# A decoder layer with attention, feature mixing and 64 experts on one core: queries copied by transfers, projection work dealt anew, and rest blocks of 64 rows with both parts in one product

## The reference: what is computed

```
x: (4, 1024, 1024) float32, ctx: (4, 1024, 512)
x = x + attention(layernorm(x))      # 16 heads of 64, causal, rotary positions
x = x + mixing(layernorm(x), ctx)    # softmax(q k^T) of ctx, applied to x (one per sequence)
x = x + experts(layernorm(x))        # 64 experts, top 8, inner width 384
# experts:
top_val, top_idx = top_k(softmax(x @ gate.T), 8)
# the lower four choices of a token may be rerouted to a similar expert that some token has among its first four
rerouted = mapping[top_idx];  rerouted[:, :4] = top_idx[:, :4]
# rows are grouped by expert, with group_sizes counted from the data
gate, up = split(ragged_dot(xs, gate_up_proj));  y = ragged_dot(silu(gate) * up, down_proj)
out[tok] += y * w
```

## Time and profile before

| what | time |
|---|---|
| median of the runs | 7708.29 us |
| the profiled execution | 7711.42 us |
| its span (first to last instruction) | 7709.8 us |
| its mean granted TensorE clock | 0.969 |

### The profile page before, as it was taken

One profiled execution on the slowest core, in us unless ns is written; L12 is line 12 of the kernel. 1 busy time (PEld: TensorE's weight loads), 2 busy tenths in 40 slices (PEclk: granted clock), 3 DMA queues, 4 the chain that ended last, 5 costly groups with the idle time before them and its releaser, 6 DMA issues.

```text
span 7709.8 us, 118231 instructions
## 1 busy us (share of the span) xinstructions
PE 7148.1 (93%) x37743; PEld 5881.9 (76%) x37744; DVE 3972.6 (52%) x7056; ACT 3523.7 (46%) x6510; POOL 1815.6 (24%) x1602
## 2 busy tenths in 40 slices
PE   7998888898996899995799999999999999999999
PEld 5776776776775778784688888888888888888887
DVE  5666667666665443445444444444444444444444
ACT  4666676666665222120244444444444444444443
POOL 1122113113110000000233333333333333333333
PEclk9999999999998999996899999999999999999999
DMA  2111111112111222221465555556556565556555
GB/s 66 45 55 51 44 55 51 44 45 60 45 46 58 79 69 85 76 67 36 123 176 170 161 161 161 161 161 165 161 155 165 161 181 160 159 163 162 162 161 150
DMA packets 303596, 858.60 MB, mean 111 GB/s; under 512 B 42080, under 2 KB 83552, under 8 KB 303328
## 3 DMA queue, kind: packets, MB, share of 16 engines
q0 software_dynamic: 98928, 365.58, 20.3%
q1 hardware_dynamic: 204400, 489.67, 19.5%
HBM read 614.84 MB, written 206.70 MB: 107 GB/s over the span
## 4 chain that ended last, share of the span: by engine, by line
PE 52%; DVE 0%; POOL 0%; issue 0%; DMA 0%; ACT 0%; DVEq 0%; POOLq 0%
PE ps_gu L1932 10%; PE ps_gu L1934 10%; PE ps_gu L1933 10%; PE ps_y L1932 5%; PE ps_y L1934 5%; PE ps_y L1933 5%; PE ps_xe L1952 3%; PE ps_xe L1961 1%; PE ps_l L1941 1%; PE ps_h L2044 0%; DVE logits L2206 0%; DMA x_rows<-rows,gather_s 0%; DVE xs_lo L2252 0%; DVE at_hi L2199 0%; POOL x_rows L1869 0%
## 5 line engine op out<-in xcount | busy, mean ns | idle before, releaser
L1932 PE MATMUL ps_gu<-xs_hi,gu_hi 128*128 128x512 f32 x3072 | 1213.5, 395 | 7.3 <-DVE gu_lo L2291 7.3
L1934 PE MATMUL ps_gu<-xs_hi,gu_lo 128*128 128x512 f32 x3072 | 1207.0, 393 | 0.0
L1933 PE MATMUL ps_gu<-xs_lo,gu_hi 128*128 128x512 f32 x3072 | 1204.4, 392 | 0.0
L1911 POOL TENSOR_TENSOR dn_lo<-raw_w,dn_hi 128x512 fp32r<-128x512 f32 x384 | 485.0, 1298 | 947.0 <-ACT dn_hi L2114 947.0
L1932 PEld LDWEIGHTS ps_gu<-xs_hi,gu_hi 128*128 128x128 f32 x3072 | 577.8, 188 | 130.4 <-DVE gu_lo L2291 7.7
L461 PE MATMUL ps_qkv<-xt_hi,w_hi 128*128 128x512 f32 x1512 | 639.8, 423 | 37.7 <-ACT proj L614 30.0
L1933 PEld LDWEIGHTS ps_gu<-xs_lo,gu_hi 128*128 128x128 f32 x3072 | 578.1, 188 | 124.8
L1934 PEld LDWEIGHTS ps_gu<-xs_hi,gu_lo 128*128 128x128 f32 x3072 | 577.6, 188 | 125.3
L1932 PE MATMUL ps_y<-dn_hi,hs_hi 128*128 128x512 f32 x1536 | 628.6, 409 | 0.0
L893 DVE TENSOR_TENSOR pt_lo<-ps_t,pt_hi 128x512 fp32r<-128x512 f32 (+3 forms) x768 | 426.6, 555 | 391.9 <-ACT pt_hi L713 376.9
L644 ACT ACTIVATE probs<-ps_s,neg_max 128x128 f32<-128x128 f32 (+7 forms) x512 | 379.5, 741 | 506.6 <-DVE neg_max L824 505.7
(11 more groups left out here) (326 smaller groups left out, 15577.1 us busy)
## 6 DMA issues: line engine op xcount, KB each, us to landing
raw_w<-w_gu SPq DMA_DIRECT2D x384, 512.0 KB, 4.2
raw_w<-w_down SPq DMA_DIRECT2D x192, 512.0 KB, 6.3
w_raw<-wqkv SPq DMA_DIRECT2D x192, 256.0 KB, 2.7
turned<-proj SPq DMA_DIRECT2D x512, 64.0 KB, 2.0
out<-residual SPq DMA_DIRECT2D x36, 512.0 KB, 2.6
attn_out<-out_t POOLq DMA_DIRECT2D x128, 128.0 KB, 2.3
residual<-x SPq DMA_DIRECT2D x32, 512.0 KB, 5.3
stage<-attn_out SPq DMA_DIRECT2D x32, 512.0 KB, 5.8
```

Of the source, the lines that this page charges most:

```text
L1911: pool.tensor_tensor(dn_lo[:, f, a], raw_w[:, f, a], raw(dn_hi[:, f, a]), ALU.subtract).then_inc(dn_lo_ok, 1)
L1932: pe.matmul(out, a_hi, w_hi, start=first, stop=False)
L1933: pe.matmul(out, a_hi, w_lo, start=False, stop=False)
L1934: return pe.matmul(out, a_lo, w_hi, start=False, stop=last)
```

## The change

**Attention.**

- `twin_queries` moves from VectorE to the SP queue: two transfers from `q_hi` to `q_hi` for each half of the queries, ordered at the step in which ScalarE rounds them. `split_queries` waits for both.
- A table `SHARE` says how many of the 144 projection matmuls stand in each of the 24 steps, in place of six in each. A chain can end at other steps (`ended`), and the emptying of the bank and the rotation's transfers follow it.
- The fourth query block of each unit (`ON_DVE = (3,)`) is multiplied with its reciprocal by VectorE, directly after the reciprocal, and no more by ScalarE. TensorE waits on two semaphores for a unit.
- The other tables are changed. SP's and GpSimd's lists are made from the tables step by step.

**Experts.**

- Rest blocks have 64 rows (`T = P // 2`). Their number is counted anew: the part of ceil(count / 64) above 8. The held operand has the high parts of the 64 rows in its first 64 columns and the low parts in the other 64 (`xt`, `ht`), so a product is two matmuls: with the high and with the low weights. The result has two halves of 64 partitions, and they are added: for gate and up ScalarE copies the lower half out (`lower_rows`) and VectorE adds (`add_rows`). To the second layer's output both halves are added in `out`: by `send_last` for the first 64 partitions and `send_second` for the others, which waits until the first has landed.
- The table has each rest block's row numbers twice (`finish_list`); `scatter_n`, `scatter_l` and `scatter_m` hold them for the sends (`place_last`).
- In a rest block the second layer's first part stands before the third transpose, and ScalarE's and VectorE's third h behind the next tail's rows.
- ScalarE splits the first two chunks of the next expert's weights before it reads the counts (`first_weights`).

```diff
@@ self_attention
-    PER = NS // NC
+    TERMS = 3 * HB
...
-    SCALED_AT = {False: (5, 9, 15, 18), True: (5, 9, 17, 21)}
-    ADDED_AT = {False: (6, 10, 16, 19), True: (6, 10, 18, 21)}
-    HI_AT = {False: (6, 10, 16, 20), True: (6, 10, 18, 21)}
-    LO_AT = {False: (7, 11, 17, 21), True: (7, 11, 19, 22)}
-    TWIN_AT = {False: {15: 1, 22: 3}, True: {15: 1, 22: 3}}
-    V0_AT = {False: 21, True: 15}
-    V1_AT = 3
-    W_AT = {4: (1, 4), 5: (1, 5), 18: (2, 0), 19: (2, 1), 22: (2, 2), 23: (2, 3)}
+    SHARE = {False: [6, 6, 6, 6, 5, 3, 9, 7, 6, 6, 6, 6, 11, 13, 2, 6, 5, 2, 5, 4, 7, 6, 6, 5], True: [8, 8, 8, 6, 6, 6, 6, 6, 6, 6, 6, 8, 7, 9, 6, 6, 6, 6, 4, 4, 4, 4, 4, 4]}
+    SCALED_AT = {False: (4, 8, 13, 17), True: (5, 10, 14, 20)}
+    ADDED_AT = {False: (5, 10, 14, 19), True: (6, 11, 17, 20)}
+    HI_AT = {False: (6, 10, 17, 19), True: (7, 11, 20, 21)}
+    LO_AT = {False: (7, 11, 18, 20), True: (8, 12, 21, 21)}
+    V0_AT = {False: 23, True: 15}
+    V1_AT = 1
+    W_AT = {2: (1, 4), 6: (1, 5), 15: (2, 0), 18: (2, 1), 22: (2, 2), 23: (2, 3)}
     XN = GQ
-    X_AT = {6: ((13, 14), (16, 17), (18, 19), (20, 22)), 7: ((2, 3), (4, 5), (6, 7), (8, 9))}
+    ON_DVE = (3, )
+    X_AT = {6: ((12, 13), (16, 17), (18, 19), (20, 23)), 7: ((0, 3), (4, 5), (6, 7), (8, 9))}
...
+            def twin_queries(j, p, n):
+                half = chains_of(p)[turns_of(p)[n]][1]
+                a = slice(half * HALF, half * HALF + HALF)
+                sp.wait_ge(qk_hi_ok, START + j * 4 + n + 1)
+                sp.dma_start(raw(q_hi[HD:P, 0, a]), raw(q_hi[0:HD, 0, a])).then_inc(twin_ok, 16)
+                sp.dma_start(raw(q_hi[0:HD, 1, a]), raw(q_hi[HD:P, 1, a])).then_inc(twin_ok, 16)
...
+                if i in ON_DVE:
+                    dve.wait_ge(inv_ok, START + j * NQ + n + 1)
+                    stand_alone(dve, passed)
+                    dve.tensor_scalar(probs[g][:, i, 0:keys], probs[g][:, i, 0:keys], inv_sum[:, n:n + 1], 1.0,
+                                      ALU.mult, ALU.mult).then_inc(norm_late, 1)
@@ experts
+            def send_second(n):
+                pool.wait_ge(yl_sent, LOADED + n * 32 + 16)
+                stand_alone(pool, passed)
+                pool.indirect_dma_start(out, bass.IndirectOffsetOnAxis(ap=scatter_m[:, 0:1], axis=0), y_last[T:P, :], None,
+                                        compute_op=ALU.add).then_inc(yl_sent, 16)
...
+            def packed_product(out, a, w_hi, w_lo, first, last):
+                both = a.rearrange("p a t -> p (a t)")
+                pe.matmul(out, both, w_hi, start=first, stop=False)
+                return pe.matmul(out, both, w_lo, start=False, stop=last)
...
+            def place_last(n):
+                dve.wait_ge(yl_sent, LOADED + n * 32)
+                dve.wait_ge(wl_ok, START + n + 1)
+                stand_alone(dve, passed)
+                dve.tensor_copy(scatter_m[:, :], scatter_n[T:P, :])
+                dve.tensor_copy(scatter_l[:, :], scatter_n[:, :]).then_inc(sl_ok, 1)
...
             def tail_block(e, t):
+                def add_rows(f):
+                    dve.wait_ge(tlow_ok, START + t * FB + f + 1)
+                    dve.tensor_tensor(gu_sum[:, f % 2, :], ps_gu[0:T, f % 2, 0:W], gu_low[:, f % 2, :], ALU.add).then_inc(tsum_ok, 1)
...
                 gather_tail_index(e + 1 + t, (e + 1) * SUP + t + 1)
+                place_last(e + 1 + t)
+                add_rows(0)
                 multiply(0)
+                add_rows(1)
                 multiply(1)
                 rest_of_h(0)
+                add_rows(2)
                 multiply(2)
                 rest_of_h(1)
-                rest_of_h(2)
...
                 keep_tail_weights(e + 1 + t, e)
                 rest_of_tail(e + 1 + t)
-                dve.wait_ge(yl_sent, LOADED + (e + t + 2) * 16)
-                stand_alone(dve, passed)
-                dve.tensor_copy(scatter_l[:, :], table[:, bass.ds((e + 1) * SUP + t + 1, 1)]).then_inc(sl_ok, 1)
+                rest_of_h(2)
```

More of the change, by code:

```diff
@@ L156, in at_border, with share, ended @@
         return p % NP >= NP - 2
+    def share(p, s):
+        before = sum(SHARE[at_border(p)][:s])
+        return [(n // TERMS, n % TERMS) for n in range(before, before + SHARE[at_border(p)][s])]
+    def ended(p, s):
+        return [c for c, n in share(p, s) if n == TERMS - 1]
     def chains_in(p):
@@ L353, in attention @@
-                if exists(j + 2):
-                    load_w(j + 2, p + 2, 4)
-                    load_w(j + 2, p + 2, 5)
-            for_pairs(sp, lambda: None, attention, lambda: None)
+                for s in range(NS):
+                    if not last:
+                        for n in range(4):
+                            if s == HI_AT[border][n] and chains_in(p)[turns_in(p)[n]][0] == Q:
+                                twin_queries(j + 1, p + 1, n)
+                    if more and p == NP - 2:
+                        for t in range(GQ):
+                            if s == X_AT[p][t][1]:
+                                load_next(b, t + XN)
+                    if s in W_AT:
+                        ahead, i = W_AT[s]
+                        ahead, i = (ahead, i + RAWS) if i + RAWS < NC else (ahead + 1, i + RAWS - NC)
+                        if exists(j + ahead):
+                            load_w(j + ahead, p + ahead, i)
+                    if not last:
+                        for c in ended(p, s):
+                            if c in turns_in(p):
+                                turn_halves(j + 1, c, turns_in(p).index(c))
@@ L358, in _, with prologue @@
+            def prologue():
+                turn_halves(0, 0, 0)
+                turn_halves(0, 1, 1)
+                twin_queries(0, 0, 1)
+                turn_halves(0, 3, 2)
+                load_w(1, 1, 0)
+                load_w(1, 1, 1)
+                turn_halves(0, 4, 3)
+                twin_queries(0, 0, 3)
+                for i in range(RAWS, NC):
+                    load_w(1, 1, i)
+            for_pairs(sp, prologue, attention, lambda: None)
             for k in range(RAWS):
@@ L551, in attention @@
                         scores(j + ahead, (slot + ahead) % 2, unit, i)
-                    if 0 < s and place < PER - 1:
+                    if 0 < s and not done:
                         weigh_values(j, slot, s - 1, base + tiles["probs", s - 1] + 1)
@@ L733, in attention @@
                         fresh.append((j + ahead, unit, i))
-                    if s in hi_at and not last:
-                        split_qk(j + 1, p + 1, 1 - slot, hi_at.index(s))
-                    if place == PER - 1 and not last:
-                        empty_bank(j + 1, p + 1, c, ps_qkv)
+                    if not last:
+                        for c in ended(p, s):
+                            empty_bank(j + 1, p + 1, c, ps_qkv)
+                        for n in range(4):
+                            if s == hi_at[n]:
+                                split_qk(j + 1, p + 1, 1 - slot, n)
             def drain():
@@ L1704, in _ @@
             dve.tensor_copy(hi16[:, 0:E, :], part[:, :, :])
-            after(dve.tensor_scalar(count[:, :], count[:, :], P - 1, None, ALU.add))
+            after(dve.tensor_scalar(count[:, :], count[:, :], P // 2 - 1, None, ALU.add))
             after(dve.tensor_scalar(part[:, :, :], rank[:, :, :], P - 1, None, ALU.bitwise_and))
```

286 lines of the change are left out of this document (129 added, 157 removed).

## The result

| | us, median | ratio to before, 95% interval |
|---|---|---|
| before (runs beside it) | 7707.65 | |
| after | 7606.56 (7605.61 to 7607.82) | 0.9867 [0.985, 0.9884] |
| forecast | 7538, range 7430 to 7640 | |

It became faster by 101 us, inside the range and at 0.6 of the forecast gain. The profiled executions differ by 104.9 us of span (7709.8 and 7604.9).

The account below looks back on a forecast made before the run. TensorE was taken as the bound: full in the experts' stage, 252 us idle on waits in attention. Attention -132 and experts -38 make -170, from 7711.4 to 7541, 7538 at the median's level; range 7430 to 7640.

Parts of the forecast that it names:

- The copy: Attention: query copies move from VectorE to SP; TensorE's stall -90 us, clock's fall -32, late border copy +7.
- The border's +7: Two last pairs of a sequence: second query copy, ordered at 21, about 1 us late in 7 pairs, +7 us.
- Normalising: Attention: VectorE normalises each unit's fourth block; waits for probabilities -27 us, for the emptied bank -15, for pt_lo +10.
- The lock: Attention: ports shared by VectorE and GpSimd; w_lo meeting the moved normalisation at steps 3 and 15 costs +15 us.
- Dealing: Attention: projection matmuls dealt unevenly over the steps change only which wait is covered; 0 us, bounds -60 and +60.
- The experts: Experts' stage: 36 packed rest blocks for 31 -81 us, third-h stall +22, result sends +18, end +3; sum -38.
- (b): Rest blocks: VectorE's low part of the third h comes late, 0.6 us stall in each of 36, +22 us.
- (c): Rest blocks' two sends in turn: a following full block is covered, a following rest block waits, 6 x 3 = +18 us.
- End: End of the span: two half sends in turn add 0 to 6 us, taken as +3.
- 1: Rival: attention's stall moves on, lock at steps 3 and 15, pt_lo waits up a quarter; 7621 us, chance 0.20.
- 3: Rival: attention's copies late behind SP's other orders, TensorE waits 9 to 10 us; 7826 us, chance 0.05.
- 4: Rival: attention's twin waits and clock as before, the experts' gain spent on its own waits; 7705 us, chance 0.05.

Follow-up runs that it names:

- experiment 11: The changed kernel with even dealing in steady pairs and the fourth block normalised on ScalarE again; 7634.3 us, ratio 0.9900.
- experiment 4: The changed kernel with the fourth block of each unit normalised on ScalarE again; 7639.6 us, ratio 0.9904.
- experiment 10: The changed kernel with even dealing in steady pairs and other rotation and rounding steps in the two last pairs of a sequence; 7561.2 us.
- experiment 8: The changed kernel with six projection products in each step of steady pairs again; 7578.5 us, ratio 0.9832.
- experiments 2 and 9: Changed kernel with third h rounded and subtracted before the next tail's rows, 7585.9 us; the same plus TensorE's late second count and earlier third transpose, 7560.7 us.

## Why the prediction was right in sign and short in size

**The copy, -90 - 32 + 7 = -115: too large.** The stall went as described, but the term was costed as if what is next had room. Alone the copy is worth 48 us: 28 of idle time in place of 90, and 21 of busy time beside the 32 for the clock. The prediction did say that V's part and the low queries are moved out of the way; that belongs to the price, and with those and the other moved tables the step comes to some 75: experiment 11, which has the copy, the tables and even dealing, stands 73 below before. The border's +7 was 18.0 us of wait in seven pairs (15.6 in six, and 2.4 put down to issue on the same line). From ScalarE's rounding to the landing it took 4.1 us, less than the 6.4 of the prediction; but from the start of step 21 to the need it is 3 us there and not 5.2, and ScalarE begins 1.4 us into them.

**Normalising, -27 - 15 + 10 = -32: right in sum under the dealing that was built**, 33 measured (56 under even dealing). Its terms were -33, -14 and +19, and smaller waits and the clock make up the rest. But before this move the waits for the probabilities stood at 81 us in experiment 4, not at the 54.9 of the earlier trace rows, so in the changed kernel, at 48, they are hardly below before.

**The lock, +15: nothing that can be seen on the new operation.** It is never longer:

```profile
L827 DVE TENSOR_SCALAR probs<-probs,inv_sum 128x1024 f32<-128x1024 f32 x64 | 48.2, 753 | 9.6 <-DVE inv_sum L821 0.3
L827 DVE TENSOR_SCALAR probs<-probs,inv_sum 128x512 f32<-128x512 f32 x64 | 31.1, 486 | 9.6 <-DVE inv_sum L821 0.2
```

In the 27 cases in which it overlaps a w_lo it had begun first, and there the w_lo is the longer one: 1.56 to 1.58 us beside the operation on 1024 keys, where the median of all is 1.29. By the Trainium skill (SBUF — State Buffer, SBUF: two separate sides) whoever starts first has the shared ports and the other waits; the trace agrees, here and at the other end: at 572.19 above, L778 begins while the w_lo of 571.90 (1.48 us) runs, and takes 1.75 instead of 0.69. So the meetings took place, but in the order that costs VectorE nothing; the prediction had named another cover, that the w_lo would be past by then. Elsewhere in attention such meetings got fewer: before, 92 operations of VectorE with two SBUF sources began inside a w_lo and lasted 59 us in sum beyond their usual 0.69, after it are 34 with 29 us. What that is worth to TensorE isn't shown.

**Dealing, 0 within -60 and +60: +28 with the normalising on VectorE, +5 (not told from nothing) without it.** The steps don't add: from experiment 11's -73 one comes to the -101 of the changed kernel by +5 and -33, or by -56 and +28. With +28 this is the step of attention that failed, and with it a change that the prediction named nowhere: the rotation is scaled one step earlier (4 for 5, and 14 for 17 in border pairs, whose chain ends earlier too), which makes VectorE wait for the transfer, 104 us instead of 30, with pt_lo behind it. At the border, moving the rotation's steps back (experiment 10) took 2.9 us a pair off the wait before step 16. For steady pairs no kernel was run with step 5 again, so that the early scaling itself costs something there is argued from the timeline; experiment 8 shows that most of what stood at steps 5, 6 and 17 went by even dealing, with the early scaling left as it was. With even dealing alone a steady pair is at the 68 us that was forecast.

**The experts, -38: +6.6.** Blocks: 35 at the shortest, 10.34, are 362 against 431.5 us for the 31 of before, -69.6, with some of the stall (b) in it (0.1 to 0.3 us instead of 0.6); the prediction's -81 + 22 = -59 for 36 blocks. (c) 5 blocks behind a rest block at +1.9, without the wait at their end: +9.3 against +18; small stalls in the 30 others +5.7. End +5.9 against +3. Not foreseen: 30 waits of TensorE for its queue, 52.9 - 8.2 = +44.7, and the clock's falls behind them: full blocks sum to 3548.3 us instead of 3537.7, +10.6. -69.6 + 9.3 + 5.7 + 5.9 + 44.7 + 10.6 = +6.6. The step that failed is (c)'s "Covered" for a full block behind a rest block: it followed ScalarE and the weights, not TensorE's own queue. The rows for it were in the trace of before: 2.5 us of queue records in front of the next block, hidden by the 14 of the 18 second-layer products of 0.233 us that followed the last release (3.5 us, median). The packed form leaves 12, and the moved low part sets the last wait in front of the last 4, 0.9 us.

One such fall: TensorE at the head of a full block behind a rest block, 4.0 us at a mean granted clock of 0.58, a mixture of 1.2 and 2.4 GHz, after an idle time of 1.7 us:

```profile
4177.00:4181.00 4.00, 3.85 (x10) 3.06 (x11) 2.16 (x8) 2.90 (x6) 1.29 (x1) 0.58 0.74 238
```

**The rivals.** 1 names the nearest time, 7621. Its waits for pt_lo nearly doubled, not by the lock: 19 us came with VectorE's new operation, as it had said, and the rest with the tables and the dealing. 3, SP's order, struck nowhere in steady pairs. 4's half, the experts' gain spent on its own waits, came true: -38 became +6.6.

**The prediction's own signs.** Both of its signs of being wrong appeared: attention's idle time stayed at 202 us, above the 180 that it named, and the experts' stage is as long as before. Of the signs for its terms, the bank's wait more than halved, but the probabilities' didn't, the clock of attention is 0.98 and not 0.99, and the copy's wait is 15.6 us, not under 15. That attention as a whole came to -115 beside a forecast of -132 is in part luck: the copy gave less than half of its 115, moved tables that had no term of their own gave some 25, and half of the gain is busy time at a higher clock, where the prediction had a quarter. The time fell inside the range, but the sum that led there didn't hold.

With the dealing even, the border's steps and the queue mended, the change gives 7516.5, 191 us below before: more than the forecast's 170, but by edits that the prediction didn't price.

## What to carry to other kernels

Where work at the end of a loop is cut, look at the engine's queue as at an engine: from its last wait to the next block's first instruction it has branches and reads to do, and only instructions that stand behind that wait hide them. An operation that waits for a transfer on an in-order engine should stand as late as its user allows, since all that is behind it waits too; where it must stand early, keep enough of the other engine's work beside it. And a removed stall is worth what is left when the next wait in the final order is counted: price it together with what is moved beside it.

## What the runs showed of the hardware that was not expected

- Reading one block count into TensorE's queue takes 0.29 to 0.54 us, 0.75 with the records around it; with branches, two counts and set-up it is 2.6 to 3.2 us (median 2.7) from the end of the operation that releases the last products to the next block's first, and 1.9 with one count moved away.
- The profile names as releaser a semaphore that came before the queue was there: 45 us stood under a VectorE line that had no part in them.
- The order on GpSimd matters by kind: VectorE's operations with two SBUF sources take 1.5 to 1.75 us when they begin inside a w_lo (two SBUF sources), but 0.67 to 0.76 in 18 cases inside the layer norm's tensor_scalar of 3.8 to 4.3 us (the rotation's L777, L778 and L783 and the low parts of L791, L792 and L795); one line, L796, took 1.43 us there in three cases, which I can't explain.
- Executions of one attention code start the experts up to 13 us apart (3613.7 to 3627.1, experiments 2 and 9), so single profiles tell what lies ahead of the experts apart only beyond that.
